# A second PSUM bank for the attention-weighted sums, taken from the ring of a one-core decoder layer

## What is computed

```python
x = x + self_attn(layernorm(x))            # 2 heads of 64, rope, causal
x = x + cross_attn(layernorm(x), ctx_1024) # 16 heads of 8, 1601 context rows, softmax over 1601
x = x + ffn(layernorm(x))                  # 128 -> 512 -> 128, gelu, plus a low-rank term of 16 tokens
```

## Time and profile before

| | us |
|---|---|
| median of 3 runs | 372.27 |
| lowest and highest run | 370.23, 373.81 |
| the profiled execution's own time | 371.86 |
| its span, first to last instruction | 370.0 |

### The profile page before, as it was taken

One profiled execution on the slowest core, in us unless ns is written; L12 is line 12 of the kernel. 1 busy time (PEld: TensorE's weight loads), 2 busy tenths in 40 slices (PEclk: granted clock), 3 DMA queues, 4 the chain that ended last, 5 costly groups with the idle time before them and its releaser, 6 DMA issues.

```text
span 370.0 us, 11883 instructions
## 1 busy us (share of the span) xinstructions
PE 342.8 (93%) x4811; PEld 158.1 (43%) x4817; DVE 296.1 (80%) x601; ACT 294.7 (80%) x598; POOL 123.5 (33%) x202
## 2 busy tenths in 40 slices
PE   7669789998999999999999999999989999998986
PEld 3432233544545445444534445433433344443445
DVE  3779989698997997799899987999978879790023
ACT  1644269988898798998898898998987999799762
POOL 3510755497020206799300133383000036100000
PEclk9999899999999999999999999999998999999999
DMA  7535495034310331135302022023020101000001
GB/s 234 210 105 156 152 277 203 4 136 168 113 57 2 111 96 46 59 135 185 125 28 80 2 80 59 3 58 135 13 77 2 54 29 58 17 2 3 16 2 30
DMA packets 20010, 30.72 MB, mean 83 GB/s; under 512 B 1432, under 2 KB 17218, under 8 KB 19956
## 3 DMA queue, kind: packets, MB, share of 16 engines
q1 hardware_dynamic: 19956, 29.97, 25.5%
HBM read 18.62 MB, written 11.34 MB: 81 GB/s over the span
## 4 chain that ended last, share of the span: by engine, by line
PE 44%; DVE 13%; ACT 13%; POOL 12%; issue 7%; DMA 7%; SPq 3%; ACTq 0%; DVEq 0%; POOLq 0%
PE wsum L1177 15%; PE ring L1146 10%; PE ring L1192 9%; DVE part_max L773 9%; ACT probs L991 6%; PE ring L1214 6%; DMA q_unit<-consts 5%; POOL k_parts L618 3%; ACT q_unit L1001 3%; POOL k_rest L658 2%; POOL k_parts L663 2%; DMA q_rows<-q_parts 2%; ACT prob_self L1037 1%; SPq L518 1%; SPq L561 1%
## 5 line engine op out<-in xcount | busy, mean ns | idle before, releaser
L773 DVE TENSOR_REDUCE part_max<-ring 128x1 f32<-128x512 f32 x384 | 238.3, 681 | 25.6 <-PE ring L1214 24.3
L991 ACT ACTIVATE probs<-ring 128x512 f32<-128x512 f32 (+1 forms) x416 | 222.0, 601 | 29.4 <-PE ring L1192 26.1
L1177 PE MATMUL wsum<-probs,v_aug 128*32 128x256 f32 (+1 forms) x1664 | 134.0, 390 | 3.4 <-ACT unit_ctx L995 3.1
L1192 PE MATMUL ring<-q_unit,k_unit 51*128 51x256 bf16 (+1 forms) x832 | 126.5, 274 | 3.9 <-ACT probs L991 1.9
L1214 PE MATMUL ring<-k_unit,q_unit 51*128 51x512 bf16 x384 | 118.7, 386 | 4.2 <-DMA q_unit<-consts 1.5
L1192 PEld LDWEIGHTS ring<-q_unit,k_unit 51*128 51x128 bf16 (+1 forms) x832 | 44.6, 96 | 97.2 <-issue 76.1
L1177 PEld LDWEIGHTS wsum<-probs,v_aug 128*32 128x32 f32 (+1 forms) x1664 | 38.7, 109 | 40.6 <-issue 33.9
L1214 PEld LDWEIGHTS ring<-k_unit,q_unit 51*128 51x128 bf16 x384 | 34.1, 93 | 16.2 <-issue 4.8
L618 POOL TENSOR_TENSOR max_parts<-neg_max,c_sb 128x8 bf16<-128x8 f32 x16 | 3.3, 208 | 111.6 <-DVE neg_max L781 111.3
L1001 ACT ACTIVATE q_unit<-ring 3x512 bf16<-3x512 bf16 x32 | 18.6, 580 | 1.7 <-PE ring L1231 1.5
L790 DVE RECIPROCAL unit_rsum<-ring 128x8 f32<-128x8 f32 x16 | 3.2, 198 | 20.4 <-PE ring L1239 20.4
(11 more groups left out here) (132 smaller groups left out, 333.1 us busy)
## 6 DMA issues: line engine op xcount, KB each, us to landing
k_unit<-k_rows SPq DMA_DIRECT2D x30, 300.2 KB
ctx_sb<-ctx_t SPq DMA_DIRECT2D x3, 800.5 KB, 8.2
k_rows<-k_parts SPq DMA_DIRECT2D x3, 601.5 KB, 3.3
k_rows<-k_parts SPq DMA_DIRECT2D x3, 599.2 KB, 3.3
even<-ffn_rows SPq DMA_DIRECT2D x3, 512.0 KB, 3.6
q_unit<-q_rows SPq DMA_DIRECT2D x30, 48.0 KB
k_rows<-k_parts SPq DMA_DIRECT2D x3, 401.0 KB, 4.1
k_rows<-k_parts SPq DMA_DIRECT2D x3, 399.5 KB, 4.1
```

The costliest lines, as they stand in the source:

```text
L773: v_.tensor_reduce(part_max[:, par, q, head, hp, c:c + 1], ring[s][:, 0:MW], AX.X, ALU.max)\
L991: a_.activation(probs[0:rows, i % PB, :], ring[s][0:rows, :], ACT.Exp).then_inc(drained[s], 1)
L1177: last = mm(wsum[32 * j:32 * j + 32, 0:S], v_aug[0:rows, v // UB % 3, at:at + 32], probs[0:rows, i % PB, S * (j // 2):S * (j // 2 + 1)], s ...
L1192: last = mm(ring[s][0:keys, S * hp:S * (hp + 1)], k_unit[rows, u, L * hp + P * t:L * hp + P * t + keys], q_unit[rows, u, hp, :], start=Tru ...
```

## The change

The sums get two banks, `wsum[0]` and `wsum[1]`; unit `v` uses `wsum[v % 2]`. The ring has 6 banks instead of 7. TensorE's first sums of unit `v` wait for the copy of unit `v - 2` instead of that of unit `v - 1`. `keep` writes to `wsum[0]`. The order of `PLAN` and all tables stay as they are; since `ring_slots` counts with `NR`, each ring item now waits for the one 6 ring items before it.

```diff
-NR = 7
+NR = 6
...
-        wsum = ctx.enter_context(nc.psum_tensor("wsum", [P, 512], F32))
+        wsum = [ctx.enter_context(nc.psum_tensor(f"wsum{i}", [P, 512], F32)) for i in range(2)]
...
             def unit_sums(v):
                 act.wait_ge(pv_done, KT * (v + 1))
-                a_.activation(unit_ctx[:, :], wsum[:, 0:S], ACT.Copy).then_inc(unit_ctx_done, 1)
+                a_.activation(unit_ctx[:, :], wsum[v % 2][:, 0:S], ACT.Copy).then_inc(unit_ctx_done, 1)
...
             def keep(n):
                 for _ in range(n):
-                    mm(wsum[:, :], still[:, 0:P], still[:, :], start=True, stop=True)
+                    mm(wsum[0][:, :], still[:, 0:P], still[:, :], start=True, stop=True)
...
-                    if v:
-                        pe.wait_ge(unit_ctx_done, v)
+                    if v > 1:
+                        pe.wait_ge(unit_ctx_done, v - 1)
...
-                    last = mm(wsum[32 * j:32 * j + 32, 0:S], v_aug[0:rows, v // UB % 3, at:at + 32],
+                    last = mm(wsum[v % 2][32 * j:32 * j + 32, 0:S], v_aug[0:rows, v // UB % 3, at:at + 32],
```

## The result

| | before | changed |
|---|---|---|
| median (us) | 372.50 (6 runs) | 378.13 (6 runs) |
| lowest and highest | 370.23, 375.57 | 376.96, 379.36 |
| profiled execution, its span | 371.86, 370.0 | 378.04, 376.1 |

The ratio is 1.0149, with a 95% interval of 1.0113 to 1.0184: the change costs 5.6 us. The direction and the range were right. The forecast of 381.0 was 3 us too high, and the expected loss (9.1 us) was over half as large again as the measured one. What remains to be explained is which term was too big, and what the new bank was worth.

A forecast was written before the change was run, and what follows sets the result against it. TensorE, swinging with its nearly as slow readers over the ring, was taken as the bound. 371.9 + 13.0 (ring loss) - 1.5 (queries' DMA wait) - 2.4 (second sums bank) = 381.0 us, range 375.5 to 388.

The forecast's parts named there:

- What bounds the kernel: TensorE, 93% busy, alternates with nearly as slow readers, VectorE and ScalarE (80% each); the ring carries them through.
- The places: Unit ends (0.56 us late) and self-attention row maxima on VectorE (1.04 to 1.66 us) carry most of the ring lateness.
- The second bank's gain: At each unit's first sums, TensorE no longer waits for ScalarE's copy: 2.4 us gained, between 0 and 3.5.
- elsewhere the slack is about 0.24 us: Outside units 4, 8 and 15, seven units' first sums were counted as gaining 0.24 us each.
- The ring's loss: Six banks for seven make 144 of 979 ring items late: 13.0 us lost, at most 21.3.
- the give-back: Delays falling into waits TensorE had anyway cost nothing: 10.5 of 15.6 us left at least; up to 1.5 absorbed at queries' DMA.
- If every shift is worth only what the last late item of its stretch shows: Low estimate over the 64 late stretches of ring items: 10.5 us of loss left.
- The middle between two bounds: The ring loss was set at 13.0 us, between estimates of 10.5 and 15.6 us.
- The signs: Profile: copy wait gone, TensorE's waits for `probs`, `part_max`, `q_unit` over 10 us, readers' idle up about as the span.
- Depth not needed: Rival, 11%: ring lateness falls nearly always into existing TensorE waits; loss of 3 to 4 us, time 371 to 372 us.
- Full price: Rival, 10%: all 21.3 us of ring lateness are paid and the new sums bank gains nothing: 393 us.
- The clock rival: Rival, 13%: more TensorE waits bring half-clock falls, 1.2 us each, two to five times more often: 383 to 387 us.

The follow-up runs named there:

- experiment 10: All eight PSUM banks in one pool shared by ring and sums, given out oldest first, against the kernel before: 371.01 us, ratio 0.9976.
- the trial against it: Changed kernel plus two matmuls of zeros after step 1 of unit 0, to keep TensorE busy before 56 us: 378.68 us, ratio 1.0188 to the kernel before.
- experiment 5: Kernel before, with each unit's first sums (from unit 1 on, except 11) moved from step 3 to step 4: 373.60 us, ratio 1.0038.
- experiments 1: Kernel before with six ring banks instead of seven, still one sums bank, one PSUM bank unused: 378.86 us, ratio 1.0195.

## Why the prediction was right or wrong, point by point

- **What bounds the kernel: right.** TensorE and its readers swing, and the ring is what the swing lives on. With one sums bank, the time falls by 18.8 us from the ring of five (397.64) to six (378.86) and by 6.5 to seven (372.37).
- **The places: right.** The late pairs that were read off the old trace are where TensorE waits in the new one, as far as these two places show: 1.07 us measured for 1.04 read in unit 8's row maxima, 0.49 for 0.56 at unit 7's start.
- **The second bank's gain: mis-sized.** It was put at 2.4 us. In the changed kernel 1.1 us were kept by the traces (0.7 by the medians, 1.6 at the same clock). The step that failed is "elsewhere the slack is about 0.24 us", for which the prediction shows no row, and the 0.7 us counted for unit 15. The seven units with such slack kept 0.7 us of 1.7 and unit 15 kept 0.3 of 0.7; the lead was handed back at the next bank that wasn't free, at the turn of step 4 or within four steps. With the full ring depth (experiment 10) it was kept in units 3, 12, 13, mostly in 7, and 0.8 us in 15. With five banks it was nothing.
- **The ring's loss: mis-sized.** It was put at 13.0 us less 1.5. The kernel with six ring banks and nothing else measured 6.5 us (378.86 against 372.37). Subtracting its trace from the one before at the first scores of each step, all rises of the shift, the opening's and those under its own fall of the clock (57.6 to 61.1) included, sum to 11.8 us, inside the bounds of 10.5 and 15.6 that were given; but there are also falls of 5.2 us, and the forecast had 1.5 for them. (A finer grid gives larger sums of both kinds, so that the rises fit the bounds is in part luck; the difference, 6.6 us, doesn't hang on it.) The step that failed is the give-back. Of the falls, 1.2 are the waits for the queries' DMA (units 2, 6 and 10), 1.0 the waits for GpSimd's split of the maxima (units 1 and 5), which the sum left out, 0.7 the fall of the clock at 278 us that this kernel's profiled execution didn't have; the rest are pieces of up to 0.44 us, which were not traced one by one. The waits of TensorE say the same: its loads of M items wait 15 us more in the changed kernel, its loads of scores 5.3 us less. "If every shift is worth only what the last late item of its stretch shows" was meant as the lower end and wasn't one, since behind the last late item TensorE often stood before the same reader's next read, late or not, as at 190.15.
- **The middle between two bounds: wrong choice.** Both bounds leaned the same way, as neither took the old waits in, though the lower one was meant to.
- **The signs.** The wait for the copy is gone, TensorE's loads of M items wait over 10 us for VectorE and nearly that for ScalarE, and the readers' idle time grew by 6.9 us, about as much as the span: as said. Two signs failed: the waits for `q_unit` did not grow (4.3 and 4.2 us), and those of the scores fell.
- **The rivals.** "Depth not needed" fell: 5.6 us are clear of it. "Full price" fell too. The clock rival: the changed kernel's profiled execution has one more fall, behind the longest new wait. The timed runs price one at 1.0 to 1.4 us, as was worked out (1.2). It happened once more, not two to five times. It belongs to the short ring: all five traces with six banks and the full row maxima have a fall that begins between 56.1 and 58.8 us, and no trace with seven or more banks has one there. But it is a small part of the 5.6 us: at the same clock the changed kernel is still 5.4 us slower (4.7 to 6.1). And the two rings of five, which wait most, have mean clocks of 0.979 to 0.991, no lower than the rest. The Trainium skill (TensorE: Matmul & The Clock Gate, A second HAM failure mode: psum-queue depth-cycling) describes idles between matmul groups so frequent that the clock keeps swinging between its two levels. Such a swing didn't come here: TensorE's waits on the ring rose at dozens of places, and the clock fell once more.
- **Rotating banks.** The Trainium skill (Perfetto Trace Analysis, Matmuls) wants independent matmul groups to rotate through different banks, so that reading one overlaps the next. The ring of this case bears that out (6.5 us for its seventh bank); for an accumulation that is swapped 15 times it gained 0.7 to 1.6 us at a ring of six and nothing at a ring of five.
- **Open.** How the rest of the loss splits over its places was not settled: shorter row maxima took 1.5 us out of units 4 and 8, and hardly anything out of the distance at the same clock. How much of unit 0's 1.6 us is its own fall of the clock is open as well, as the trial against it did not remove the fall; the two kernels with short row maxima, neither of which has a fall there, still add 1.5 us in unit 0.

## What to carry to other kernels

A buffer that several engines drain in turn is worth most where it has nearly no slack left: before taking one away, subtract the reads from the next uses in the old trace, then subtract the waits that the producer has at the same places anyway, on every engine and DMA it waits for. The first subtraction gave the two places that were looked up to 0.1 us here, the second decides how much of it is paid. A wait that is removed gains only what the next full buffer lets through; and a bank that is needed for a moment can be shared with the ring instead of split off it. And before two medians a microsecond apart are compared, compare the runs at the same granted clock.

## What was not expected of the hardware

- One fall of the granted clock to 0.50 costs 1.0 to 1.4 us of 378, read off six timed runs that differ in nothing else (376.96 at a mean of 0.991, 378.04 to 378.33 at 0.986, 379.36 at 0.982), and it comes and goes between executions of one program. A difference of about a microsecond between two medians can be this alone, as in experiment 5, or can be hidden by it, as in experiments 1 and 10.
- Apart from it, two executions of different kernels agree step by step to about 0.01 us where their order and waits are the same: in experiment 10, for instance, the shift stays at 0.12 to 0.14 us from unit 0 to step 8 of unit 2. Traces resolve effects that the timed medians can't, at the price of being one execution each.
